# A graph network with a mixture of experts: x loaded in the tables' stage, wide compares, a second helper at the gather, an elu split between two engines

## What is computed

```python
def _gcn_conv(x, src, dst, W, b, n):
    deg = jax.ops.segment_sum(jnp.ones_like(dst, jnp.float32), dst, n)
    dinv = jax.lax.rsqrt(jnp.maximum(deg, 1.0))
    norm = dinv[src] * dinv[dst]
    h = x @ W
    out = jax.ops.segment_sum(h[src] * norm[:, None], dst, n)
    return out + b
...
h = jax.nn.relu(_gcn_conv(x, src, dst, W_gcn, b_gcn, n))
h = _batch_norm(h, g0, beta0)
h = _gat_conv(h, src, dst, W1, a_src1, a_dst1, b1, n)
h = jax.nn.elu(_batch_norm(h, g1, beta1))
h = _gat_conv(h, src, dst, W2, a_src2, a_dst2, b2, n)
h = jax.nn.elu(_batch_norm(h, g2, beta2))
...
x = x + gnn(layernorm(x), edges)
x = x + ffn(layernorm(x))          # top 2 of 8 experts
```

## Time and profile before

| what | us |
|---|---|
| median of the runs | 8200.73 |
| profiled execution | 8197.49 |
| its span | 8195.7 |
| PE busy in the span | 4762.8 |
| DVE busy | 4741.7 |
| ACT busy | 1656.0 |
| POOL busy | 5058.8 |

### The profile page before, as it was taken

One profiled execution on the slowest core, in us unless ns is written; L12 is line 12 of the kernel. 1 busy time (PEld: TensorE's weight loads), 2 busy tenths in 40 slices (PEclk: granted clock), 3 DMA queues, 4 the chain that ended last, 5 costly groups with the idle time before them and its releaser, 6 DMA issues. The chain is left out here.

```text
span 8195.7 us, 142425 instructions
## 1 busy us (share of the span) xinstructions
PE 4762.8 (58%) x25109; PEld 3791.4 (46%) x25110; DVE 4741.7 (58%) x12098; ACT 1656.0 (20%) x7006; POOL 5058.8 (62%) x5345
## 2 busy tenths in 40 slices
PE   3434343343345666666666666665656656779994
PEld 2333333333334444444444454444444444559993
DVE  7822222222226777777777777777777778764445
ACT  3500000000003111111111231111111112653331
POOL 0077777777773777777777337777777774015552
PEclk9999999999997778778777787788787777869997
DMA  5511111111114555555555245555555553412226
GB/s 182 175 28 28 28 28 28 28 28 27 28 26 132 138 137 137 137 137 137 137 137 137 73 125 138 137 137 137 136 136 136 136 135 93 139 48 70 70 70 217
DMA packets 517844, 846.44 MB, mean 103 GB/s; under 512 B 138006, under 2 KB 363486, under 8 KB 510540
## 3 DMA queue, kind: packets, MB, share of 16 engines
q0 software_dynamic: 229376, 543.89, 26.4%
q1 hardware_dynamic: 274522, 284.12, 11.9%
q10 hardware_dynamic: 13298, 12.80, 0.4%
HBM read 750.77 MB, written 82.11 MB: 102 GB/s over the span
## 5 line engine op out<-in xcount | busy, mean ns | idle before, releaser
L727 POOL DMA_INDIRECT gat_rows<-gat_table,gat_idx x3278 | 3103.1, 947 | 1060.7 <-issue 954.0
L838 PE MATMUL gat_ps_sum<-gat_msg,gat_hot 128*128 128x260 f32 x6656 | 2299.6, 505 | 1212.2 <-DVE feat L857 1208.0
L838 PEld LDWEIGHTS gat_ps_sum<-gat_msg,gat_hot 128*128 128x128 f32 x6656 | 1580.1, 249 | 1562.0 <-DVE gat_msg L893 1222.8
L727 POOL DMA_INDIRECT gcn_rows<-gcn_table,gcn_idx x1639 | 1546.8, 944 | 850.5 <-issue 499.2
L838 PE MATMUL gcn_ps_sum<-gcn_rows,gcn_hot 128*128 128x64 f32 x3328 | 813.1, 426 | 1260.1 <-issue 661.7
L838 PEld LDWEIGHTS gcn_ps_sum<-gcn_rows,gcn_hot 128*128 128x128 f32 x3328 | 741.3, 328 | 1331.9 <-issue 808.6
L857 DVE SCALAR_TENSOR_TENSOR feat<-gcn_ps_sum,in_first,feat 128x64 f32 x416 | 118.0, 284 | 1606.5 <-PE gcn_ps_sum L838 1606.5
L821 PEld LDWEIGHTS gat_ps_near<-gat_tab,gat_hot_t 128*128 128x128 bf16 x6656 | 271.9, 101 | 789.4 <-issue 612.6
L821 PE MATMUL gat_ps_near<-gat_tab,gat_hot_t 128*128 128x24 bf16 x6656 | 310.8, 178 | 457.3 <-DVE gat_hot L869 453.6
L893 DVE TENSOR_TENSOR gat_msg<-gat_rows,gat_ps_as 128x1024 f32<-128x1024 f32 x416 | 503.5, 1210 | 116.1 <-issue 115.3
L869 DVE TENSOR_TENSOR gat_hot<-gat_count,mod_t 128x512 f32<-128x512 f32 x832 | 566.5, 681 | 0.0
(11 more groups left out here) (307 smaller groups left out, 6414.2 us busy)
## 6 DMA issues: line engine op xcount, KB each, us to landing
gat_mod<-mod_rows SPq DMA_DIRECT2D x832, 128.0 KB
gat_ahead<-gat_table SPq DMA_DIRECT2D x6400, 1.0 KB
gi_mods<-mod_rows SPq DMA_DIRECT2D x52, 1024.0 KB, 4.7
gat_rows<-gat_table,gat_idx POOLq DMA_INDIRECT x3278
gcn_ahead<-gcn_table SPq DMA_DIRECT2D x3200, 0.2 KB
gcn_rows<-gcn_table,gcn_idx POOLq DMA_INDIRECT x1639, 2.4
gat_table<-feat SPq DMA_DIRECT2D x28, 910.0 KB, 4.3
mix_rows<-y_rows SPq DMA_DIRECT2D x98, 256.0 KB, 5.1
```

The source lines that it names most:

```text
L727: pool.indirect_dma_start(B["rows"][:, j, k, :], None, table, bass.IndirectOffsetOnAxis(ap=B["idx"][:, j, k:k + 1], axis=0)).then_inc(rows ...
L838: mm = pe.matmul(B["ps_sum"][b][:, 0:width], B["hot"][:, j, k, :], rhs, start=(k == 0), stop=(k == CH - 1))
```

## The change

Four parts, in four stages:

1. Five of the seven batches of x, and the tail, are loaded by ACT's queue in the edge tables. The first two stay with SP in the GCN's input, since the tables use their place in `feat` as scratch. DVE's memset of the last windows, which x waits for, becomes its first instruction of the tables; the statistics take batches 2 to 6 first.
2. DVE's six compares with sums become one compare of 3072, two adds in bf16 that halve each group's row, and one reduce of the remaining 128 columns per group. These four steps of an octet are spread over four turns. SP's wait for a free `gi_mods` counts octets now. ACT writes its second step into `away` itself.
3. A second helper, only at the GCN's edges: in the group of 16 with number 9, ACT fetches the fourth chunk as SP does in number 2, 25 chunks in all. Its turn is push, stage (four ahead), bring, fetch.
4. In the second GAT layer's input ACT makes the straight part (`straight`), two more activations a turn, and DVE's `line` goes.

```diff
-AHEAD, AT = 16, 2
+AHEAD = 16
+ATS = (2, 9)
...
+def load_x(eng, K, S, x, b):
+
+    w0, w1 = b * S.WB, min((b + 1) * S.WB, S.NW - 1)
+    eng.dma_start(K["feat"][:, w0:w1, 0:FEAT],
+                  x[w0 * P:w1 * P, :].rearrange("(w p) f -> p w f", p=P)).then_inc(K["x_in"][b], 16)
+    if b == S.NB - 1:
+        eng.dma_start(K["feat"][0:S.TAIL, S.NW - 1, 0:FEAT], x[(S.NW - 1) * P:S.N, :]).then_inc(K["x_in"][b], 16)
...
+    K["late_x"] = -(-3 * NT * GE // (S.WB * WIDE))
...
+            @block.scalar
+            def _(act):
+                act.wait_ge(cleared, 1)
+                for b in range(K["late_x"], S.NB):
+                    load_x(act, K, S, x, b)
...
+                dve.memset(K["feat"][:, S.NW - 1:S.NWP, :], 0.0).then_inc(cleared, 1)
...
-                sp.wait_ge(cleared, 1)
-                for b in range(NB):
-                    w0, w1 = b * WB, min((b + 1) * WB, NW - 1)
-                    sp.dma_start(feat[:, w0:w1, 0:FEAT],
-                                 x[w0 * P:w1 * P, :].rearrange("(w p) f -> p w f", p=P)).then_inc(x_in[b], 16)
-                sp.dma_start(feat[0:TAIL, NW - 1, 0:FEAT], x[(NW - 1) * P:N, :]).then_inc(x_in[NB - 1], 16)
+                for b in range(late):
+                    load_x(sp, K, S, x, b)
...
-                    wait(sp, counted, MINE * (o - (RING - 1)))
+                    wait(sp, counted, o - (RING - 1))
...
-                for b in range(NB):
+                for b in [*range(late, NB), *range(late)]:
...
+                def matches(i, c):
+                    o, b = RING * i + c, c % 2
+                    dve.wait_ge(mods_in[c % RING], 16 * (i + c // RING + 1))
+                    wait(dve, halved[0], o - 1)
+                    dve.tensor_scalar(folds[0][:, b, :, :], mods[:, c % RING, 0:MINE, :], K["part"][:, 0:1], None,
+                                      ALU.is_equal).then_inc(counted, 1)
+
+                def halve(n):
+
+                    def step(i, c):
+                        o, b, half = RING * i + c, c % 2, GE >> n
+                        dve.wait_ge(halved[n - 2] if n > 1 else counted, o + 1)
+                        wait(dve, halved[n] if n < 2 else tallied, o - 1)
+                        have = folds[n - 1][:, b, :, :]
+                        dve.tensor_tensor(folds[n][:, b, :, :], have[:, :, 0:half], have[:, :, half:2 * half], ALU.add
+                                          ).then_inc(halved[n - 1], 1)
+                    return step
+
+                def tallies(i, c):
                     o = RING * i + c
-                    dve.wait_ge(mods_in[c % RING], 16 * (i + c // RING + 1))
-                    wait(dve, counted, MINE * o)
-                    for q in range(MINE):
-                        dve.tensor_scalar(equal[:, q, :], mods[:, c % RING, q, :], K["part"][:, 0:1], 0.0,
-                                          ALU.is_equal, ALU.add,
-                                          accum_out=K["tally"][:, one(EIGHT * o + q)]).then_inc(counted, 1)
-
-                pace(dve, NW // 2, [(puts, 1), (counts, 0), (takes, 0)], RING)
-                for o in range(NW // 2, NO):
-                    counts(o // RING, o % RING)
+                    dve.wait_ge(halved[1], o + 1)
+                    dve.tensor_reduce(K["tally"][:, bass.ds(EIGHT * o, MINE)], folds[2][:, c % 2, :, :], AX, ALU.add
+                                      ).then_inc(tallied, 1)
+
...
+                pace(dve, NO, [(puts_some, 1), (tallies, -3), (halve(2), -2), (halve(1), -1),
+                               (matches, 0), (takes_some, 0)], RING)
...
-                        ins = act.activation(same[:, q - MINE, :], away[:, q - MINE, :], ACT.Relu, scale=-1.0,
+                        ins = act.activation(away[:, q - MINE, :], away[:, q - MINE, :], ACT.Relu, scale=-1.0,
...
-            for k in range(CH - ahead(i, c)):
+            for k in range(CH - len(ahead(i, c))):
...
+    def helper(eng, h):
+
+        at, own = ats[h], ats[h] % RING
+        regs = [eng.alloc_register(f"{L}row{h}_{r}") for r in range(BURST)]
+        count = (NG - 1 - at) // AHEAD
+
+        def known(n):
+
+            return not isinstance(n, int) or n < count
+
...
+        def fetch(i, c):
+
+            n, b, part = 2 * i + c // AHEAD, c // AHEAD % 2, c % AHEAD
+            if not known(n):
+                return
+            if part == 0:
+                wait(eng, pushed[h], 16 * (n - 1))
+                eng.sem_inc(ahead_free[h], 1)
+                eng.wait_ge(idx_in[h][b], 16 * (i + c // AHEAD // 2 + 1))
+                eng.sem_inc(ahead_free[h], 1)
+            eng.load(regs, B["ahead_idx"][0:1, h, b, part * BURST:(part + 1) * BURST])
+            for r in range(BURST):
+                p = part * BURST + r
+                row = eng.snap(regs[r], min_val=0, max_val=S.N - 1)
+                eng.dma_start(B["ahead"][p:p + 1, h, b, :], table[bass.ds(row, 1), :]).then_inc(ahead_in[h][b], 16)
+
+        def push(i, c):
+
+            n, b = 2 * i + c // AHEAD, c // AHEAD % 2
+            if c % AHEAD == at - 1 and known(n):
+                eng.wait_ge(ahead_in[h][b], 16 * P * (i + c // AHEAD // 2 + 1))
+                eng.sem_inc(ahead_free[h], 1)
+                wait(eng, rows_used, AHEAD * n + (AHEAD + at - 3))
+                eng.dma_start(B["rows"][:, own, CH - 1, :], B["ahead"][:, h, b, :]).then_inc(pushed[h], 16)
+        return bring, fetch, push
...
-        pace(act, NG, [(weigh, 2), (stage, RING + 2)] if gat else [(stage, RING)], AHEAD)
+        if gat:
+            pace(act, NG, [(weigh, 2), (stage, RING + 2)], AHEAD)
+        else:
+            bring, fetch, push = helper(act, 1)
+            pace(act, NG, [(push, -AHEAD), (stage, RING), (bring, AHEAD), (fetch, 0)], 2 * AHEAD)
...
-                turns(NQ, [(clip, 0), (line, 1), (unite, 0)] if elu else [(line, 0)])
+                turns(NQ, [(clip, 0), (unite, 0)] if elu else [(line, 0)])
...
+                def straight(q):
+                    wait(act, staged, q - (SLOTS - 1))
+                    for k in range(KP):
+                        ins = act.activation(some(shf, q, k), feat[:, four(q), k * P:(k + 1) * P], ACT.Identity,
+                                             scale=scale[:, k:k + 1], bias=shift[:, k:k + 1])
+                    ins.then_inc(shifted, 1)
+
...
-                turns(NQ, ([(expo, 2)] if elu else []) + [(place, 0)])
+                turns(NQ, ([(expo, 2), (straight, 2)] if elu else []) + [(place, 0)])
```

More of the change, by code:

```diff
@@ L449, in build_gcn_input @@
         mods = T.sb("gi_mods", [P, RING, EIGHT, GE], BF16)
-        equal = T.sb("gi_equal", [P, MINE, GE], BF16)
+        folds = [T.sb(f"gi_fold{n}", [P, 2, MINE, GE >> n], BF16) for n in range(3)]
         away = T.sb("gi_away", [P, EIGHT - MINE, GE], BF16)
-        same = T.sb("gi_same", [P, EIGHT - MINE, GE], BF16)
         less_p = T.sb("gi_less_p", [P, 1])
@@ L745, in mods @@
                          ).then_inc(mod_in[j], 16)
-        def bring(i, c):
-            n, b = 2 * i + c // AHEAD, c // AHEAD % 2
-            if c % AHEAD == 0 and known(n):
-                at = (AHEAD * n + AHEAD + AT) * GE + (CH - 1) * P
-                sp.dma_start(B["ahead_idx"][0:1, b, :], src[bass.ds(at, P)].rearrange("(a e) -> a e", a=1)
-                             ).then_inc(idx_in[b], 16)
-        def fetch(i, c):
-            n, b, part = 2 * i + c // AHEAD, c // AHEAD % 2, c % AHEAD
-            if not known(n):
-                return
-            if part == 0:
-                wait(sp, pushed, 16 * (n - 1))
-                sp.sem_inc(ahead_free, 1)
-                sp.wait_ge(idx_in[b], 16 * (i + c // AHEAD // 2 + 1))
-                sp.sem_inc(ahead_free, 1)
-            sp.load(regs, B["ahead_idx"][0:1, b, part * BURST:(part + 1) * BURST])
-            for r in range(BURST):
-                p = part * BURST + r
-                row = sp.snap(regs[r], min_val=0, max_val=S.N - 1)
-                sp.dma_start(B["ahead"][p:p + 1, b, :], table[bass.ds(row, 1), :]).then_inc(ahead_in[b], 16)
-        def push(i, c):
-            n, b = 2 * i + c // AHEAD, c // AHEAD % 2
-            if c % AHEAD == AT - 1 and known(n):
-                sp.wait_ge(ahead_in[b], 16 * P * (i + c // AHEAD // 2 + 1))
-                sp.sem_inc(ahead_free, 1)
-                wait(sp, rows_used, AHEAD * n + (AHEAD + AT - 3))
-                sp.dma_start(B["rows"][:, own, CH - 1, :], B["ahead"][:, b, :]).then_inc(pushed, 16)
         pace(sp, NG, ([(mods, 0)] if gat else []) + [(bring, AHEAD), (fetch, 0), (push, -AHEAD)], 2 * AHEAD)
@@ L782, in act_program @@
         regs = [act.alloc_register(f"{L}act_w{j}") for j in range(RING)]
+        per = 1 if gat else 2
         def stage(i, c):
-            j, g = c % RING, AHEAD * i + c
+            j, g = c % RING, per * AHEAD * i + c
             used = c - RING
-            wait(act, rows_in[j], landed(i, used))
-            if ahead(i, used):
-                wait(act, pushed, 16 * (i + used // AHEAD))
```

(12 more changed lines are left out.)

62 lines of the change are left out of this document (39 added, 23 removed).

## The result

The changed kernel takes 8130.48 us, median of four runs (8128.7 to 8130.9); the kernel before took 8201.12 beside it. The ratio is 0.9915, 95% interval 0.9902 to 0.9927. That is 70.6 us less; 56 were forecast, and 8130 lies in the range of 8110 to 8190.

A forecast was written before the change was run, and what follows sets the result against it. Bounds by stage: the list wait (tables), VectorE (GCN's input), POOL (GCN's edges), TensorE (elu, then ACT). Terms +3 − 39 − 31 + 11 = −56 gave a median of 8145 us, range 8110 to 8190.

The forecast's parts named there:

- Part 1, +3: Edge tables and GCN's input: 11 us of waits and memset removed, lists delayed by 14; between −11 and +14.
- the delay of the lists: Edge tables: x loads share the one DMA engine carrying the lists, which land 14 us later, between 0 and 25.
- +20 for equal shares: Edge tables: if lists and x get equal time on the engine, the lists come about 20 us later.
- the full 25 us: Edge tables, a rival: the lists wait for all moved x loads; part 1 is +14, time 8156, chance 0.12.
- Part 2, -39: GCN's input: VectorE's octet falls by 0.74 us, 52 times; −62 with fast adds, +24 with slow ones.
- the overlap of neighbours: GCN's input: neighbouring VectorE steps overlap by 0.063 us; four such overlaps bring 3.51 us down to 3.26.
- Part 3, -31: GCN's edges: POOL's gathers fall from 1639 to 1614, 25 × 1.2487 us saved, if ACT keeps up.
- The turn of ACT: GCN's edges: ACT's fetches, register load, index copy, further DMAs and waits take 4.5 us, 0.3 under POOL's turn.
- The rival's 477 against 373 ns: GCN's edges: ACT issues slower than SP and becomes the bound; chance 0.07 up to 5.01 us a turn, 0.08 over.
- the point of decision, 4.84: GCN's edges: POOL's turn of 16 groups takes 4.84 us; a longer ACT turn makes ACT the bound.
- Part 4, +11: Second attention layer's elu: ACT becomes the bound, 24 turns of 4.0 us instead of 3.56; from +8 to +20.
- The 0.46 a turn of the working: Second attention layer's elu: time each of 24 turns was to lengthen once ACT, not TensorE, is the bound.

The follow-up runs named there:

- e6: The changed kernel with each list's last 103 rows loaded as 96 and 7, nothing else: 8108.47 us, ratio 0.989.
- e9: The changed kernel with ACT, at the GCN's edges, fetching one of its eight rows a turn a second time into a spare buffer: 8132.5 us, ratio 0.9913.
- e10: The changed kernel with ACT, at the GCN's edges, fetching four of its eight rows a turn twice: 8459.08 us, ratio 1.031.
- e4: The changed kernel with part 4 undone, so VectorE makes the straight part again: 8118.84 us, ratio 0.9903.
- e1: The changed kernel with part 1 undone, all of x loaded by SP in the GCN's input again: 8131.79 us, ratio 0.9917.

## Why the prediction was right, point by point

**Part 1, +3, measured +1.75.** The step that decided was the delay of the lists, put at +14 between 0 and +25: it was 13.75, and rows of the two queues do alternate on the one engine. That it came within 0.25 us is luck in part: alternation alone was worked out at +11, and +14 was taken between it and +20 for equal shares. What the other 2.75 us are made of no run separates. The Trainium skill, "DMA: Bandwidth & Descriptors", section "Issuing engines are not separate DMA queues", says that DMAs of different issuing engines interleave on the same sixteen engines. They do here; that the lists would lose the full 25 us by it was my reading, and they lost about half of that.

What the working did not ask is why one engine carried the lists. The share of 0.06 in the earlier trace rows was read as a given, and it was the largest thing to be had in this stage (e6). The same page of the Trainium skill has the answer in the section "Why a DMA increments its semaphore by 16 and not by 1": the engines used are the largest number up to 16 that divides the row counts. By that rule 103 rows go to one engine and 96 to sixteen; the runs agree (a share of 0.06 for the 103 rows, and win_i at 19.20 instead of 33.79 once they are split). Nor did the working ask what else stands in SP's queue ahead of the list's last piece.

**Part 2, -39, measured -43.65** (the first gather's -41.90 less part 1's 1.75). The kind of each cost was right: the adds were put at 0.95 and 0.55 us and took 0.950 and 0.548, the reduce 0.95 and 0.944, and ACT's share of the octet stayed covered. Mis-sized were the compare (1.06, in fact 1.01) and the overlap of neighbours: 0.063 a step was taken from the old compares; here steps follow by 0.08 less than they last (130.69 to 131.55 where the reduce lasts 0.94). An octet is 4.03 instead of 4.16, 52 x 0.13 = 6.8 us more gained; 1.6 of it did not arrive, perhaps for filling and emptying the four turns, which no run separates. By the Trainium skill, "VectorE: DVE Perf Modes", section "The perf-mode tier table (the rule you actually need)", the estimate for the adds was 0.96 and 0.56; the trace bears it out within about 2%.

**Part 3, -31, measured -31.22.** The step of a gather, 1.2487 us, did not change in its last digit. The turn of ACT was put at 4.5 and takes 4.21. Of the 0.29, 0.06 is the register load (722 ns where SP's took 782), 0.06 the eight DMAs (217 ns each where SP's take 225), and 0.15 are the two further DMAs and the waits, which the turn shown doesn't have. The rival's 477 against 373 ns did not carry over to a DMA of one row; leaving it aside for SP's own fetches was right, though why those medians differ was not tested. e9 and e10 bear out the point of decision, 4.84: a turn of 4.52 costs nothing, one of 5.46 does.

**Part 4, +11, measured +8.71** in the gap between the two GATs' gathers, 6.9 by e4's. All four places are short once ACT is the bound (1.08 us), the lower end of what was worked out: 3.90 a turn, not 4.0, and 24 times the 0.34 over TensorE's 3.56 are 8.2. (The 0.46 a turn of the working is 0.44 by its own figures, 10.6 in place of 11.)

**What no step had**: -1.50 ahead of the first GAT and -3.10 in both GATs' edges together, which the change doesn't touch. The first GAT's edges took 2062.9 and 2063.2 us in the two traces without part 1 (the kernel before and e1), 2066.5 to 2069.7 in the eleven with it; the second's took 2072.3 and 2073.5 without it, 2061.7 to 2068.8 with it. So the shift goes with part 1, which edits nothing there; why, and whether more than two traces without it would agree, stays open. With the 4.65 us of part 2, 2.29 of part 4, 1.25 of part 1 and 0.22 of part 3, less 0.22 at the end, these 4.60 are the 12.8 by which the trace's -68.8 went beyond -56. Those 4.60 came without any step of the working, and the misses of the four parts all point the same way. One reading of the earlier trace rows is off and nothing hangs on it: a slice is 205 us, so POOL is busy from about 410 us on, not from 200.

## What to carry to other kernels

A transfer that is moved under a wait competes with what that wait is for: look first at how many DMA engines the awaited transfer uses, since one with an awkward number of rows holds one engine, and splitting it can be worth more than the move. Look also at what stands ahead of its last piece in the queue that issues it. Before work is handed to an idle engine, make out which engine sets the pace of that stage, and add up the other engine's instructions a turn: that sum told within a few tenths of a microsecond that ACT had room at the edges and none in the elu. An unknown price is best taken from a row of the same shape on another engine rather than from another shape on the same engine.

## What the runs showed of the hardware

- A DMA of 103 rows of 2 KB ran on one engine, about 24 GB/s, while those of 104 rows were spread (the share was 0.64 from 10 to 18 us in the kernel before, 0.06 from 18 to 34); as 96 and 7 rows it no longer held the list up (win_i at 23.70 with x beside it, 19.20 without, 33.79 unsplit and without x).
- Two queues with rows for one DMA engine took turns row by row, though the rows differ in size: 40 of 2 KB and 39 of 1 KB from 38 to 43 us in the changed kernel.
- At the GCN's edges ACT issues a DMA of one row in 217 ns (median), SP in 225, and a register load of eight takes 722 ns on ACT and 783 on SP; at the GATs' edges SP's load takes 717, so that difference is not the engine's alone.
- An add of bf16 operands runs at float32's pace when only its result is float32: 1758 ns against 950 for 1536 elements.
